# Flamingo block on one core: the last pair's values and the output projection ahead of seven of nine feed-forward weight transposes, six of them split by GpSimd

## The reference, cut to what matters

```
x   = x + tanh(g0) * LN_out(attention(layernorm(x), ctx))       # Wq, Wkv, Wout, 16 heads of 64, one null key and value
h   = act_qdq(layernorm(x))                                       # one scale: max |.| over the whole tensor
up, gate = act_qdq(h @ dq(w_up).T), act_qdq(h @ dq(w_gate).T)     # dq: 4 bits in blocks of 32
o   = act_qdq(act_qdq(gate * fixed_qdq_u16(sigmoid(gate))) * up)
out = x + tanh(g1) * (o @ dq(w_down).T)
```

## Time and profile before

| | before |
|---|---|
| median of 3 runs | 560.23 us (559.73 to 560.52) |
| the profiled execution, its own time | 562.19 us |
| its span, first to last instruction | 560.0 us |
| PE / DVE / ACT / POOL busy in the span | 513.0 / 407.1 / 312.0 / 140.6 us |
| mean granted TensorE clock | 0.979 of full speed |

### The profile page before, as it was taken

The page is one execution under the profiler, slowest core; times in us unless marked ns, Lnnn a source line. Parts: engine busy times, 40 slices in busy tenths (PEclk is TensorE's granted clock), DMA queues, the critical chain, the costliest instruction groups (busy, mean ns, idle before and its releaser), DMA issues. The chain is left out here.

```text
span 560.0 us, 10769 instructions
## 1 busy us (share of the span) xinstructions
PE 513.0 (92%) x3936; PEld 455.6 (81%) x3936; DVE 407.1 (73%) x916; ACT 312.0 (56%) x961; POOL 140.6 (25%) x149
## 2 busy tenths in 40 slices
PE   2989999999999999999999999999789999608897
PEld 2968989988998998899899899887667878505797
DVE  5747877566656665765666676878676979999896
ACT  4744443644364254355435426455378569988992
POOL 1300511231121132123113113134123029920000
PEclk9989999999999999999999999999999999957999
DMA  8932000200110110020011001005001000100033
GB/s 309 310 134 77 1 1 28 69 2 1 56 37 0 56 37 0 0 80 14 0 56 37 0 1 39 1 3 169 1 19 39 0 1 0 39 0 1 1 114 112
DMA packets 18493, 25.85 MB, mean 46 GB/s; under 512 B 1232, under 2 KB 15824, under 8 KB 18464
## 3 DMA queue, kind: packets, MB, share of 16 engines
q1 hardware_dynamic: 18208, 25.17, 13.3%
q0 software_dynamic: 256, 0.30, 0.5%
HBM read 21.27 MB, written 4.19 MB: 45 GB/s over the span
## 5 line engine op out<-in xcount | busy, mean ns | idle before, releaser
L1672 POOL TENSOR_TENSOR probs<-probs,rinv 128x512 f32<-128x512 f32 x64 | 66.5, 1045 | 211.6 <-DVE rinv L1234 211.6
L886 ACT ACTIVATE probs<-bank,nmax 128x128 f32<-128x128 f32 x256 | 91.0, 381 | 25.0 <-DVE nmax L1226 25.0
L631 PE MATMUL bank<-wv,ctxT 128*128 128x512 f32 x384 | 95.0, 404 | 2.5 <-ACT qk L860 2.5
L631 PEld LDWEIGHTS bank<-wv,ctxT 128*128 128x128 f32 x384 | 72.2, 191 | 21.1 <-ACT qk L860 2.7
L623 PE MATMUL bank<-ctxT,wk 128*128 128x256 f32 x672 | 88.9, 282 | 0.0
L623 PEld LDWEIGHTS bank<-ctxT,wk 128*128 128x128 f32 x672 | 83.6, 188 | 0.0
L856 ACT ACTIVATE qk<-bank 128x256 f32<-128x256 f32 (+1 forms) x60 | 24.1, 402 | 95.2 <-PE bank L623 92.8
L1238 DVE COPY pT<-bank 128x512 f32<-128x512 f32 x64 | 41.1, 684 | 42.3 <-PE bank L690 42.1
L886 ACT ACTIVATION_READ_ACCUMULATOR probs<-bank,nmax 128x1 f32 x256 | 56.7, 221 | 0.0
L623 PE MATMUL bank<-xnT,wq 128*128 128x256 f32 x336 | 51.8, 290 | 0.1
L663 PE MATMUL bank<-wout,oT 128*128 128x256 f32 x384 | 47.3, 282 | 1.7 <-DVE oT L1243 0.9
(11 more groups left out here) (167 smaller groups left out, 917.2 us busy)
## 6 DMA issues: line engine op xcount, KB each, us to landing
craw<-in_ctx SPq DMA_DIRECT2D x8, 512.0 KB, 3.8
stage<-in_L_xattn_Wkv SPq DMA_DIRECT2D x8, 512.0 KB, 10.4
xa<-in_x SPq DMA_DIRECT2D x8, 256.0 KB, 2.7
xr<-in_x SPq DMA_DIRECT2D x8, 256.0 KB, 2.8
x_scratch<-y SPq DMA_DIRECT2D x7, 256.0 KB, 2.2
x2all<-x_scratch SPq DMA_DIRECT2D x1, 1536.0 KB, 6.9
xres<-x_scratch SPq DMA_DIRECT2D x6, 256.0 KB, 2.8
out<-yout SPq DMA_DIRECT2D x6, 256.0 KB, 2.2
```

The costliest lines, as they stand in the source:

```text
L631: last = mm(bk[:, :], ctxT[a][:, k, b * S:(b + 1) * S], wv[w][:, k, h * 512:(h + 1) * 512], start=(k == 0 and i == 0), stop=(k == KC - 1 a ...
L886: nc.scalar.activation(probs[:, p % 2, h, u, :], score_bank[p % 2][h][:, u * S:(u + 1) * S], ACT.Exp, bias=nmax[:, p % 2, h, u:u + 1], acc ...
L1672: G.tensor_tensor(probs[:, p % 2, h, :, :], probs[:, p % 2, h, :, :], rinv[:, p % 2, h, :].rearrange("p (u o) -> p u o", o=1).to_broadcast ...
```

## The change

PLAN_FINAL loses mid (F2, F3, F4) and F3 to F8: behind `values` of the last pair come F2 and W. F3, F4 and F5 are transposed by PE between the two halves of W, F6, F7 and F8 behind the second half, ahead of the first `x_transposes`. They go to PSUM banks 1, 3 and F2's. ACT copies each of the six banks once, unsplit in kind but with the same instruction, into new SBUF tiles wuf and wdf (in the place of `up`, behind x2all): three before `x_normalise(0)`, three between `x_normalise(0)` and `x_normalise(1)`. DVE's six lows go. POOL splits wuf into wu and wdf into wd, behind its lows of x: for each a copy and a subtraction of 128x1536. The statistics of group 6 on DVE move from F8 to F2. New waits: PE waits for all six copies ahead of `x_transposes(1)`, and for POOL's four steps ahead of the first up piece; ACT waits for them ahead of the first evacuation of an up piece; POOL waits for the six copies.

In the diff `late_weights` stands twice, first in PE's list and then in ACT's.

```diff
-    PLAN_FINAL = ([(["Q6"], ["Q7"]), ([], ["V01"]), (["V11"], []), (["F0", "F1"], [])], ["F2", "F3", "F4"],
-                  ["F5", "F6", "F7", "F8", "W"])
+    PLAN_FINAL = ([(["Q6"], ["Q7"]), ([], ["V01"]), (["V11"], []), (["F0", "F1"], [])], [], ["F2", "W"])
...
         x2all = sb("x2all", [P, NT, D])
+        wuf = sb("wuf", [P, KD, I])
+        wdf = sb("wdf", [P, KI, D])
...
+        def late_bank(i):
+            return (bank[1], bank[3], unit_bank[parity(NG - 1, FINAL.index("F2"))])[i % 3]
...
+            def late_weights(i):
+                if i == 5:
+                    unit_read(NG - 1, FINAL.index("F2"))
+                wait(pe, wt_out, i - 5)
+                weight_transposes(i, late_bank(i)).then_inc(wt_done, 1)
...
                         if last_group and b == 0:
                             last.then_inc(w_first, 1)
+                            for i in range(3, 6):
+                                late_weights(i)
...
+            for i in range(6, 9):
+                late_weights(i)
             for t in range(NT // 2 - 2):
+                if t == 1:
+                    pe.wait_ge(wt_out, 6)
                 x_transposes(t)
...
+                        if m == 1 and tg == 0 and j == 0:
+                            pe.wait_ge(wt_split, 4)
...
-            for t in range(7):
+            def late_weights(i):
+                m, r = i // 3, i % 3
+                act.wait_ge(wt_done, i - 2)
+                dst = wuf[:, :, 2 * r * P:(2 * r + 2) * P] if m == 1 else wdf[:, 2 * r:2 * r + 2, :]
+                high(dst, late_bank(i)[:, :].rearrange("p (a s) -> p a s", a=2)).then_inc(wt_out, 1)
+            for i in range(3, 6):
+                late_weights(i)
+            x_normalise(0)
+            for i in range(6, 9):
+                late_weights(i)
+            for t in range(1, 7):
                 x_normalise(t)
...
+            act.wait_ge(wt_split, 4)
             for q in range(4):
                 gu(1, q)
...
-                        if u == "F8":
+                        if u == "F2":
                             x2_statistics(g - 1, y[:, :, :])
...
+            pool.wait_ge(wt_out, 6)
+            for i, (raw, hi, lo) in enumerate(((wuf, wu[0], wu[1]), (wdf, wd[0], wd[1]))):
+                G.tensor_copy(hi[:, :, :], raw[:, :, :]).then_inc(wt_split, 1)
+                pool.wait_ge(wt_split, 2 * i + 1)
+                G.tensor_tensor(lo[:, :, :], raw[:, :, :], hi[:, :, :].bitcast(F32), ALU.subtract).then_inc(wt_split, 1)
             pool.wait_ge(scale_ready, 1)
```

More of the change, by code:

```diff
@@ L334, in gated_cross_attention_ffn @@
         fint_ready, fw_ready = sem("fint_ready"), sem("fw_ready")
+        wt_done, wt_out, wt_split = sem("wt_done"), sem("wt_out"), sem("wt_split")
         gm_t, gm_1, scale_ready = sem("gm_t"), sem("gm_1"), sem("scale_ready")
@@ L583, in unit_read, with weight_transposes @@
                     pe.wait_ge(unit_hi, copied(g, pos))
+            def weight_transposes(i, bk):
+                m, r = i // 3, i % 3
+                if r == 0:
+                    pe.wait_ge(fw_ready, m + 1)
+                wf = fraw[:, m, :, :].rearrange("p n w -> p (n w)")
+                for a in range(2):
+                    for b in range(2):
+                        src = ((2 * r + b) * D + a * P) if m < 2 else (b * I + (2 * r + a) * P)
+                        last = nc.tensor.transpose(bk[:, (2 * a + b) * P:(2 * a + b + 1) * P],
+                                                   wf[:, src:src + P], ident[:, :])
+                return last
+            def late_weights(i):
[3 more added lines that the diff above has]
+                weight_transposes(i, late_bank(i)).then_inc(wt_done, 1)
             def unit(g, pos):
@@ L643, in unit @@
                 elif kind[0] == "F":
[L644 to L654, removed]
+                    last = weight_transposes(int(kind[1]), bk)
                 else:
@@ L1730, in _ @@
                                 ALU.subtract).then_inc(xt_lo_pool, 1)
-            gate_c = gate[:, :, :].rearrange("p j t -> p (j t)")
-            up_c = up[:, :, :].rearrange("p j t -> p (j t)")
+            pool.wait_ge(wt_out, 6)
[3 more added lines that the diff above has]
+                G.tensor_tensor(lo[:, :, :], raw[:, :, :], hi[:, :, :].bitcast(F32), ALU.subtract).then_inc(wt_split, 1)
             pool.wait_ge(scale_ready, 1)
```

## The result

The changed kernel takes 557.55 us (median of 13 runs, 556.48 to 559.86) against 560.52 (13 runs, 559.73 to 564.04): ratio 0.994, 95% interval 0.9923 to 0.9958. The forecast was 557.8, in a range of 556.9 to 560.3; the measured time lies inside it.

A forecast was written before the change was run, and what follows sets the result against it. At the joint between attention and feed-forward layer, DVE's and ACT's chains both bound the first global maximum. Moving it from 414.07 to 411.62 takes 2.45 us off the median 560.23, giving 557.8 us, range 556.9 to 560.3.

The forecast's parts named there:

- (c): W with F3 to F5 between its halves on PE: halves 2.94 us each, blocks 0.58 each, no stall, ending at 402.61.
- (e): Transposes of x: sixth at 410.05 instead of 412.50, global maximum 1.57 us later at 411.62; gain at the joint 2.45 us.
- (a): Values of pair 3 on PE: run at 393.38 instead of 396.20 and end at 394.47.
- (b): oT and F2 after the values: group 6's statistics start near 396.53 instead of 402.01, DVE's chain 5.5 us earlier.
- (d): F6 to F8 after W: PE ends at 404.43; x_normalise(1) waits behind ACT's copy of F8, starting near 404.96.
- (f): POOL's four steps: 11.9 us, between 4.0 and 15.1, done about 445.5 before the first up piece at 448.9; cost nothing.
- (g): Everything behind the first global maximum: engine orders unchanged, so the 2.45 us shift lasts to the end.
- the POOL rival: At the wait before the first up piece, POOL becomes the bound; four steps end near 456.7, time 564.8 us; chance 0.08.
- The clock rival: Clock falls in the longer stretch of x transposes before the global maximum, costing 2.55 us: 560.3, no change; chance 0.09.
- the forecast's own sign of being wrong: At the joint, a granted clock under 1.00 between 403 and 417 was listed as showing the forecast wrong.

The follow-up runs named there:

- e1: Changed kernel with all six late blocks between W's halves, ACT copying all six before its first normalisation; ratio 0.9906 to the kernel before.
- e7: Changed kernel with POOL's four steps done twice and both waits moved to the eighth; 169.07 us from values of pair 2 to the end, against 163.97.
- e6: The changed kernel run again without edits; ratio 0.9928 to the kernel before.
- e2: Changed kernel without the four idle matmuls ahead of the first global maximum; ratio 0.9914 to the kernel before.
- e4: Kernel before with only the last pair's values moved ahead of F2, F3 and F4; ratio 1.0007 to the kernel before.
- e8: Kernel before with only group 6's statistics moved from F8's low to F2's; 171.19 us from values of pair 2 to the end, against 167.65.
- e3_between_nokeep: Changed kernel with all six late blocks between W's halves and without the four idle matmuls; ratio 0.9899 to the kernel before.

## Why the prediction was right, and where its sizes were off

The forecast said 2.45 us at the joint; in the first pair of traces it is 3.6 from the values of pair 2 on, in all three traces of the changed kernel 2.8 to 3.6, and in the medians 3.0 (the ratio's interval gives 2.4 to 4.3). The mechanism held step by step; two terms were mis-sized, in (c) to (e). That the time itself came within 0.3 us of 557.8 is in part luck: the forecast took 2.45 off the median of three runs of before, 560.23, and the 13 runs have 560.52.

One more row of the kernel before, PE's weight loads at the step from F4's transposes to the values of pair 3:

```profile
396.20 0.85 PEld L703 LDWEIGHTS bank<-pT,v 128*64 128x64 f32 x16 [0.17 <-issue]
```

- (a), (b): the statistics of group 6 start 4.18 us behind the values of pair 2; the forecast had 396.53 - 392.35 = 4.18.
- (c), (d): a block of four transposes was priced at 0.58 us, by the row of F4. In a series it costs 1.23 / 3 = 0.41 (396.93 to 398.16), and F2 ahead of W 0.42. The 0.58 held a step to the values, whose matmuls use another shape of the array (128*64); in the kernel before PE's weight loads idle for 0.17 us just there (the row above). That the change of shape is the reason is inferred from where such gaps stand; no run tries it. Six blocks (F2 to F7) at 0.16 us less bring F8's end to 402.56 - 391.53 = 11.0 instead of 12.1, and the normalisations behind it 0.97 us earlier than forecast.
- (e): from the sixth transposes to the global maximum I took 1.57 from the earlier trace rows; it is 1.42 after. In the row of before PE had probably waited a little for DVE's maximum there, whose readout ended 0.06 us ahead of 414.07. Together 1.1 us: the whole of the difference between 2.45 and the first trace's 3.6.
- (d), the loss of part of DVE's gain to ACT's order, is shown by e1: 1.84 us come back when the copies of F6 to F8 no longer wait for W's second half. DVE's idleness after is 2.27 us, forecast 3.
- (f): the copy takes 1.47 instead of 2.1, the subtraction 3.51 instead of 3.87; the sum of 10.1 lies between the bounds, under cover. e7 shows where the cover ends, and that the POOL rival's price had left out the clock, which falls behind PE's wait there.
- (g): the shift of 3.6 lasts to the end.

The clock rival's chance of 0.09 looks too low, and its price was too high. The clock fell at the joint in one of three traces of the changed kernel (e6, where the forecast's own sign of being wrong, a clock under 1.00, appears), in e2, and in e4, whose blocks still stand ahead of W. The price in e6 was 0.75 us, not 2.55: while the clock was 1.00 PE had waited 0.3 us for ACT at each pair of tokens, so that slower transposes cost less than their length, and the clock was back (1.00 in 410 to 411) before the gate pieces.

## What to carry to other kernels

Where two engines' chains end together, price both behind the change: taking work off one (DVE, 5.5 us) is worth only what the other (ACT and PE) can follow, and a copy that waits for a late producer must not stand in a queue ahead of work that is ready. Moving a step early pays only if what it holds up behind it has been taken away; e4 and e8 are two parts of this change, and alone the first gave nothing and the second lost. Durations of short PE blocks are best read from a row of several in series, not from one that borders on another kind of matmul.

## What the runs showed of the hardware

The runs' spread lies ahead of the change, and it goes with the clock between 35 and 40 us. Windows of that stretch in the kernel before, in e3_between_nokeep and in e1_between:

```profile
35.00:40.00 5.00, 4.98 (x15) 3.93 (x16) 1.02 (x2) 1.95 (x10) 0.00 (x0) 0.66 0.01 4
```

```profile
35.00:40.00 5.00, 5.00 (x23) 4.08 (x22) 1.68 (x6) 1.29 (x9) 1.49 (x2) 1.00 0.00 0
```

```profile
35.00:40.00 5.00, 4.42 (x10) 3.47 (x11) 0.69 (x1) 2.51 (x11) 0.00 (x0) 0.50 0.01 4
```

With 1.00 the values of pair 2 started at 390.1 to 390.9 (three traces), with 0.66 to 0.69 at 391.5 to 392.9 (four), with 0.50 to 0.55 at 394.0 to 394.8 (six). Why it falls in one execution and not in the next is open; nothing here was tried on the prologue.

The clock can fall during transposes with gaps and come back during transposes without gaps. Timeline of PE in e4:

```profile
406.04 0.66 PE L767 MATMUL bank<-ident,x2all 128*128 128x128 f32 x4 [0.96 <-ACT x2all L979]
...
408.00 3.84 PE L767 MATMUL bank<-ident,x2all 128*128 128x128 f32 x16 [0.33 <-ACT x2all L979]
```

W ended at 405.07, and PE idled 0.96 us and then did transposes alone, four in each 0.98 us; the clock was down from 408.06 (0.53 in that us), the transposes then filled PE without a gap, and the clock was back near 411.46 (0.77 in 411 to 412), before the first other matmul at 411.59. The Trainium skill, "TensorE: Matmul & The Clock Gate", Part 4: PE-mode transpose, says that full speed does not engage for transposes. This trace differs, and in the first trace of the changed kernel the clock stayed at 1.00 through transposes and gaps alone from 401.09 to 408.65; the measurement decides. Still, the clock fell in this stretch in three of the thirteen traces (e2, e4 and e6); why in these is open.
